# Expert answers, layer-3 projections and masks of a four-layer transformer: three stages made one, keys rotated in transposed layout

## The reference

```python
# layer 2, feed-forward: a token's expert answers, times its gate, are added
combine = gates1_s[:, None, None] * mask1[:, :, None] * loc_oh[:, None, :]
...
moe_out = jnp.einsum('sec,ecm->sm', combine, expert_out)
...
out = res_mlp_out * coef[:, :1] + moe_out * coef[:, 1:]
out = out + residual
# layer 3, attention: 16 heads of 8, rotary positions, a window of five keys
qh = (q @ Wq).reshape(Bq, Lq, N_HEADS, HDIM).transpose(0, 2, 1, 3)
kvl = kv @ Wkv
...
qh = qh * q_cos + rotate_half(qh) * q_sin
...
kh = kh * k_cos + rotate_half(kh) * k_sin
keep = (kidx[None, None, :] <= seg_id[:, :, None]) & (kidx[None, None, :] >= seg_id[:, :, None] - LOOKBACK)
scores = jnp.einsum('bhqd,bhkd->bhqk', qh, kh) * scale
scores = jnp.where(keep[:, None], scores, -jnp.inf)
attn = jax.nn.softmax(scores, axis=-1)
ctx = jnp.einsum('bhqk,bhkd->bhqd', attn, vh)
...
return out @ Wo
```

## Time and profile before

| | us |
|---|---|
| median of three runs | 3355.51 |
| profiled execution | 3358.82 |
| its span | 3357.3 |
| gather, 2532 to 2618 | 86.0 |
| tables, 2618 to 2628.4 | 10.4 |
| projections, 2628.4 to 2841 | 212.6 |
| masks and the way to the attention, 2841 to 2862 | 21 |
| attention of layer 3, 2862 to 3155 | 293 |

### The profile page before, as it was taken

How to read it: one execution, slowest core, us unless ns; L and a number is a source line. 1 busy time by engine, 2 the same in 40 slices (tenths; PEclk the granted TensorE clock), 3 DMA queues, 4 the chain that set the end, 5 groups by cost and what they waited for, 6 DMA issues and landing times. The chain is left out here.

```text
span 3357.3 us, 66661 instructions
## 1 busy us (share of the span) xinstructions
PE 2687.0 (80%) x24521; PEld 1819.8 (54%) x24556; DVE 2136.1 (64%) x5336; ACT 1249.5 (37%) x1888; POOL 441.2 (13%) x749
## 2 busy tenths in 40 slices
PE   4857599967999999999978887879790466788557
PEld 4634356645656666566645555556570355566427
DVE  6789789963555455555545777768203556789874
ACT  3658688850000000000016655545340111444264
POOL 0022200000000000000000000023216000445204
PEclk9987699988999999999987888889895677899789
DMA  3010000012121221212200000010131221000001
GB/s 87 28 58 1 11 18 13 16 51 101 51 101 51 76 76 50 101 50 79 72 8 14 14 9 9 1 34 26 50 100 50 69 56 38 3 0 0 8 0 50
DMA packets 88405, 136.92 MB, mean 41 GB/s; under 512 B 42950, under 2 KB 54598, under 8 KB 87243
## 3 DMA queue, kind: packets, MB, share of 16 engines
q1 hardware_dynamic: 80746, 114.75, 10.7%
q0 software_dynamic: 7520, 20.34, 2.0%
HBM read 117.75 MB, written 17.30 MB: 40 GB/s over the span
## 5 line engine op out<-in xcount | busy, mean ns | idle before, releaser
L1426 PE MATMUL banks<-l1f_xe,l1f_w 128*128 128x512 f32 x1024 | 486.2, 597 | 10.8 <-DVE l1f_xe L1625 10.8
L1625 DVE TENSOR_TENSOR l1f_xe<-l1f_hT,l1f_rwb 128x512 f32<-128x512 f32 x256 | 173.5, 693 | 301.2 <-PE banks L1428 278.6
L1428 PEld LDWEIGHTS banks<-l1f_w,l1f_xe 128*128 128x128 f32 x2048 | 270.7, 193 | 123.6 <-issue 123.6
L1631 DVE TENSOR_TENSOR l1f_ae<-l1f_aoT,l1f_rwb 128x512 f32<-128x512 f32 x256 | 172.8, 691 | 159.2 <-PE banks L1456 154.7
L1428 PE MATMUL banks<-l1f_w,l1f_xe 128*128 128x128 f32 x2048 | 271.6, 276 | 0.0
L1426 PEld LDWEIGHTS banks<-l1f_xe,l1f_w 128*128 128x128 f32 x1024 | 177.0, 192 | 141.1 <-issue 126.5
L1456 PE MATMUL banks<-l1f_ae,l1f_w 128*128 128x512 f32 x512 | 223.9, 596 | 1.4 <-DVE l1f_ae L1631 1.4
L1456 PEld LDWEIGHTS banks<-l1f_ae,l1f_w 128*128 128x128 f32 x512 | 96.7, 191 | 117.3 <-issue 115.1
L223 PE MATMUL banks<-consts,l3p_h 128*128 128x128 f32 x64 | 17.8, 433 | 164.8 <-DVE l3p_h L140 164.8
L214 POOL COPY x<-xn 128x512 f32 (+1 forms) x16 | 9.8, 611 | 973.2 <-DVE xn L1655 973.2
L1105 DVE TENSOR_REDUCE l2a_top<-banks 128x16 f32<-128x1024 f32 x64 | 78.4, 1224 | 65.2 <-PE banks L1052 64.7
(11 more groups left out here) (491 smaller groups left out, 6308.8 us busy)
## 6 DMA issues: line engine op xcount, KB each, us to landing
l1f_rwb<-l1f_shares SPq DMA_DIRECT2D x128, 512.0 KB, 4.5
l3p_ctx<-in_ctxT SPq DMA_DIRECT2D x32, 256.0 KB, 4.0
l0a_ctxT<-in_ctxT SPq DMA_DIRECT2D x16, 256.0 KB, 2.6
l2f_sent<-l0f_zero SPq DMA_DIRECT2D x4, 1024.0 KB, 7.0
l1a_ctxT<-in_ctxT SPq DMA_DIRECT2D x16, 256.0 KB, 2.6
l2c_ctxT<-in_ctxT SPq DMA_DIRECT2D x16, 256.0 KB, 2.6
l2e_rows<-l2f_sent SPq DMA_DIRECT2D x16, 256.0 KB, 2.8
l2f_answers<-l2e_y POOLq DMA_DIRECT2D x16, 256.0 KB, 2.7
```

The lines of the kernel that those rows point to most:

```text
L1426: pe.matmul(bank, w[:, n, e, :], xe[:, e % NB, :], start=(e == 0), stop=(e == E - 1))
L1428: last = pe.matmul(v_bank[:, D * j:D * j + D], xe[:, e % NB, P * j:P * j + P], w[:, 2, e, :], start=(e == 0 and j == 0), stop=(e == E - 1) ...
L1625: dve.tensor_tensor(xe[:, e % NB, :], hT[:, m, :], rwb[:, m, e, :], ALU.mult).then_inc(s.xe_ready, 1)
L1631: dve.tensor_tensor(ae[:, e % NB, :], aoT[:, m, :], rwb[:, m, e, :], ALU.mult).then_inc(s.ae_ready, 1)
```

## The change

The gather stage and the mask stage are taken out. Their work goes elsewhere:

- The gather, the update of x and its statistics become parts of the projections' pipeline. The DRAM tensor, the gates and the indices are allocated outside (`routed`) so that they outlive the experts' stage. The gathered rows have a ring of four groups. The root of the variance, per group, is ScalarE's (`root`), reciprocal and shift are VectorE's (`finish`), and the layer norm itself moves from VectorE to ScalarE (`norm`).
- Keys are projected as `kT` directly (weights stationary, context moving, one product of 512 columns for the keys, one for the rotated half) and rotated in that layout, with a table whose partitions are channels: `wide` is copied from the table, transposed on TensorE and copied by ScalarE into `key_trig`. The key transposes and the key store go.
- Values are projected in half columns: for each sequence two products with the same 64 tokens, one for the even and one for the odd heads, into the two halves of the partitions, and ScalarE stores them in one copy. The doubled context goes.
- The query rotation has three VectorE instructions of 128x512 instead of nine.
- All steps are written out (`behind=k.NG`), there is no hardware loop in this stage.
- POOL makes each tile's mask inside the attention (`make`), in four instructions instead of one copy.

```diff
-            pipeline(pe, k.NG, [(0, turn), (2, turn_k), (2, turn_q), (1, project)])
+            def keys(g, m):
+                pe.wait_ge(s.ctx_loaded, 16 * (g + 1))
+                wait(pe, s.k_chain, 2 * g)
+                pe.matmul(k_bank, wk[:, 0:D], ctxT[:, m % 2, :], start=True, stop=True)
+                pe.matmul(swapped_bank, wk[:, D:2 * D], ctxT[:, m % 2, :], start=True, stop=True).then_inc(s.k_psum, 1)
+
+            def values(g, m):
+                wait(pe, s.v_stored, g)
+                for q in range(SG):
+                    for p in range(2):
+                        last = pe.matmul(v_bank[64 * p:64 * p + 64, S * q:S * q + S], ctxT[:, m % 2, S * q:S * q + S],
+                                         wv[:, :].rearrange("c (a e n) -> c a e n", e=2, n=HD)[:, :, p, :], start=True, stop=True)
+                last.then_inc(s.v_psum, 1)
...
+            each_group(pe, [(0, keys), (0, values), (1, turn), (2, turn_q), (1, queries)])
...
+            def gather(g, m):
+                wait(pool, s.x_ready, g - RING4 + 1)
+                for j in range(TG):
+                    t = TG * g + j
+                    pool.indirect_dma_start(out=rows[:, m, j, :], out_offset=None, in_=kept.answers,
+                                            in_offset=bass.IndirectOffsetOnAxis(ap=kept.back[:, t:t + 1], axis=0)).then_inc(gathered[m], 16)
...
-            pipeline(act, k.NG, [(0, copy_hT), (2, store_k), (2, store_q)])
+            def root(g, m):
+                act.wait_ge(s.stats_ready, g + 1)
+                act.activation(rstd[:, m % 2, :], mv[:, m % 2, :, 1], ACT.Sqrt, bias=eps[:, 0:1]).then_inc(s.std_ready, 1)
+
+            def norm(g, m):
+                act.wait_ge(s.shift_ready, g + 1)
+                wait(act, s.hT_psum, g)
+                for j in range(TG):
+                    last = act.activation(h[:, j, :], k.x[:, TG * g + j, :], ACT.Identity, bias=shift[:, m % 2, j:j + 1],
+                                          scale=rstd[:, m % 2, j:j + 1])
+                last.then_inc(s.h_ready, 1)
...
+            each_group(act, [(1, norm), (0, store_v), (1, copy_hT), (2, store_q), (0, root)])
...
-            pipeline(dve, k.NG, [(0, norm), (1, rope_k), (1, rope_q), (1, store_v)])
+            def rope_q(g, m):
+                dve.wait_ge(s.q_psum, g + 1)
+                wait(dve, s.qT_psum, g)
+                wait(dve, s.q_roped, g)
+                src = k.banks[:, 2:4, :].rearrange("p b (t a h e) -> p (b t) a h e", t=2, a=2, e=HD)
+                for a, dst in enumerate((qr, q_part)):
+                    dve.tensor_tensor(dst[:, :, :].rearrange("p t (h e) -> p t h e", e=HD), src[:, :, a],
+                                      table[:, a, TG * g:TG * g + TG, :].unsqueeze(2).to_broadcast([P, TG, H, HD]), ALU.mult)\
+                        .then_inc(s.q_chain, 1)
+                dve.wait_ge(s.q_chain, 2 * (g + 1))
+                dve.tensor_tensor(qr[:, :, :], qr[:, :, :], q_part[:, :, :], ALU.add).then_inc(s.q_roped, 1)
...
+            each_group(dve, [(2, rope_q), (1, finish), (0, rope_k), (0, update), (0, stats)])
...
-        def copy(pool, t, par, used):
+        def make(pool, t, par, used):
             wait(pool, used, t - 1)
+            wait(pool, ready, t)
             settle(pool, k)
-            pool.tensor_copy(mask_b[:, par], masks[:, bass.ds(t, 1), :]).then_inc(ready, 1)
+            pool.tensor_tensor(away[:, :], k.count64, r.segments[:, bass.ds(t, 1)].to_broadcast([P, S]), ALU.subtract).then_inc(made, 1)
+            pool.wait_ge(made, 2 * t + 1)
+            settle(pool, k)
+            pool.tensor_scalar(far[:, :], away[:, :], float(-LOOKBACK), NEG, ALU.is_lt, ALU.mult)
+            pool.tensor_scalar(away[:, :], away[:, :], 0.0, NEG, ALU.is_gt, ALU.mult).then_inc(made, 1)
+            pool.wait_ge(made, 2 * t + 2)
+            settle(pool, k)
+            pool.tensor_tensor(mask_b[:, par], away[:, :], far[:, :], ALU.add).then_inc(ready, 1)
```

More of the change, by code:

```diff
@@ L991, in residents @@
         segments=segments and ctx.enter_context(nc.sbuf_tensor(f"{name}_segments", [P, k.NT], F32)))
-def store_v2(dve, k, r, g):
-    for p in range(2):
-        half = slice(64 * p, 64 * p + 64)
-        out = r.v2[half, bass.ds(SG * g, SG), :].rearrange("k q (j n) -> k q j n", n=HD)
-        psum = k.banks[half, 6:8, :].rearrange("k b (q j n) -> k (b q) j n", j=HD, n=2 * HD)[:, :, :, HD * p:HD * p + HD]
-        last = dve.tensor_scalar(out, psum, 0.0, None, ALU.add)
-    return last
 CORE_SEMS = ("weights x_read biased xn_ready stats_chain stats_ready mv_copied q_ready k_ready v_ready score_psum max_ready "
@@ L1926, in load, with _ @@
                 wait(sp, s.v_psum, g - 1)
-                wait(sp, s.ctx_loaded, 48 * g)
-                group = k.dram["ctxT"][:, bass.ds(g * GT, GT)]
-                sp.dma_start(ctxT[:, m, :], group).then_inc(s.ctx_loaded, 16)
-                for copy in range(2):
-                    sp.dma_start(ctx2[:, m, :, copy, :], group.rearrange("c (q n) -> c q n", n=S)).then_inc(s.ctx_loaded, 16)
-            pipeline(sp, k.NG, [(0, load)])
+                wait(sp, s.ctx_loaded, 16 * g)
+                sp.dma_start(ctxT[:, m % 2, :], k.dram["ctxT"][:, bass.ds(g * GT, GT)]).then_inc(s.ctx_loaded, 16)
+            each_group(sp, [(0, load)])
+        @block.gpsimd
+        def _(pool):
+            def gather(g, m):
[4 more added lines that the diff above has]
+                                            in_offset=bass.IndirectOffsetOnAxis(ap=kept.back[:, t:t + 1], axis=0)).then_inc(gathered[m], 16)
+            each_group(pool, [(0, gather)])
         @block.tensor
@@ L1937, in _ @@
             pe.wait_ge(s.weights, 16 * 5)
+            pe.wait_ge(s.wide_ready, 1)
+            for a in range(2):
+                last = pe.transpose(trig_bank[:, P * a:P * a + P], wide[:, a, :], k.ident)
+            last.then_inc(s.wide_psum, 1)
+            def keys(g, m):
[10 more added lines that the diff above has]
+                last.then_inc(s.v_psum, 1)
             def turn(g, m):
@@ L2071, in l3_masks @@
-def l3_masks(nc, k, r, masks):
-    with ExitStack() as ctx:
-        s = sems(nc, ctx, "l3m", "chain")
-        away = ctx.enter_context(nc.sbuf_tensor("l3m_away", [P, k.NT, S], F32))
-        far = ctx.enter_context(nc.sbuf_tensor("l3m_far", [P, k.NT, S], F32))
-        block = ctx.enter_context(nc.Block())
-        @block.vector
-        def _(dve):
-            chain = Chain(dve, s.chain)
-            chain.wait(chain.did(dve.tensor_tensor(away[:, :, :], k.count64.unsqueeze(1).to_broadcast([P, k.NT, S]),
-                                                   r.segments[:, :].unsqueeze(2).to_broadcast([P, k.NT, S]), ALU.subtract)))
-            chain.wait(chain.did(dve.tensor_scalar(far[:, :, :], away[:, :, :], float(-LOOKBACK), NEG, ALU.is_lt, ALU.mult)))
-            chain.wait(chain.did(dve.tensor_scalar(away[:, :, :], away[:, :, :], 0.0, NEG, ALU.is_gt, ALU.mult)))
-            chain.wait(chain.did(dve.tensor_tensor(masks[:, :, :], away[:, :, :], far[:, :, :], ALU.add)))
@@ new lines, in update, with stats @@
+            def update(g, m):
+                dve.wait_ge(gathered[m], 16 * TG * (g // RING4 + 1))
+                for j in range(TG):
+                    t = TG * g + j
+                    last = dve.scalar_tensor_tensor(out=k.x[:, t, :], in0=rows[:, m, j, :], scalar=kept.gate[:, t:t + 1], in1=k.x[:, t, :],
+                                                    op0=ALU.mult, op1=ALU.add)
+                last.then_inc(s.x_ready, 1)
+            def stats(g, m):
+                dve.wait_ge(s.x_ready, g + 1)
+                wait(dve, s.stats_ready, g - 1)
+                for j in range(TG):
+                    last = dve.bn_stats(bn6[:, m % 2, j, :], k.x[:, TG * g + j, :])
+                last.then_inc(s.bn_ready, 1)
+                dve.wait_ge(s.bn_ready, g + 1)
+                wait(dve, s.shift_ready, g - 1)
+                for j in range(TG):
+                    last = dve.bn_aggr(mv[:, m % 2, j, :], bn6[:, m % 2, j, :])
+                last.then_inc(s.stats_ready, 1)
@@ L2090, in phase_l3_attention @@
+            each_group(dve, [(2, rope_q), (1, finish), (0, rope_k), (0, update), (0, stats)])
+def phase_l3_attention(nc, k, kept):
     with ExitStack() as ctx:
         r = residents(nc, k, ctx, "l3", segments=True)
-        l3_projections(nc, k, r)
-        masks = ctx.enter_context(nc.sbuf_tensor("l3_masks", [P, k.NT, S], BF16))
+        l3_projections(nc, k, r, kept)
+        away = ctx.enter_context(nc.sbuf_tensor("l3_away", [P, S], F32))
+        far = ctx.enter_context(nc.sbuf_tensor("l3_far", [P, S], F32))
```

183 lines of the change are left out of this document (68 added, 115 removed).

## The result

The changed kernel took 3214.57 us (median of four runs, 3212.88 to 3218.49) against 3355.9 us before (3348.74 to 3356.46): ratio 0.9583, 95% interval 0.9572 to 0.9595. The forecast was 3193 us, with a range of 3168 to 3245; the range of its likeliest case, 3175 to 3212, was missed by 2.6 us. The sign, the mechanism and the gain of the merged stage came out; the price of the masks was twice what was forecast.

The account below looks back on a forecast made before the run. The prediction took the old projections as bound by a ring of latencies, the attention mostly by VectorE. Merged stage and barrier -178.5 us, masks +15, sum -163.5: 3358.8 becomes 3195.3 profiled, 3192 on the median's scale; predicted 3193, range 3168 to 3245.

Parts of the forecast that it names:

- likeliest case: Whole kernel: the forecast itself holds, with a time of 3175 to 3212 us; chance 0.60.
- The ring: Merged stage: query products, rotation, shift, norm, transposes and copy wait on each other in turn, 7.54 us a group against 13.3.
- Start and end: Merged stage: first query rotation about 28.3 us in, last rotation, transposes and copy 3.5; with the rounds and barrier, 178.5 saved.
- the masks' term: Attention: POOL making masks delays each of 15 joints (once in four tiles) by 1.0 us, +15 us.
- 14.9 + 3d: Attention: cycle of four tiles in us, d being POOL's added time a tile; 19.1 forecast, against 18.2 before.
- signs named: Profile after: among others, rotations 7.5 us apart, mask operations 0.25 to 0.3 each, joints 19.1 to 19.6 apart.
- (a): Attention: POOL's masks cost more, 2 to 3.5 us a tile, +45 to +110 in place of +15, about 3245; chance 0.14.
- (b): Merged stage: TensorE stays at 1.2 GHz; 3261 if in all rounds, 3216 if in a third; chance 0.10.
- (c): Merged stage: VectorE's operations stretch the gathers to 9.8 us a group, +36 us, 3229; chance 0.04.
- the rule weighed: Merged stage: VectorE's two-port copies and tensor_scalars block POOL, holding gathers only during the 6.3 us of tables.
- (d): Attention: the masks stay in POOL's slack, 3178 us; chance 0.08.
- (e): Attention: POOL's slow comparisons make it the bound of all 64 tiles; at 5.3 us a tile +235, 3415; chance 0.03.

Follow-up runs that it names:

- e9: Changed kernel with the value products issued twice in each group; 3216.37 us, ratio 0.9579 to the kernel before.
- e6: Changed kernel with the gather in a stage of its own again, ahead of the new projections; 3296.62 us, ratio 0.9828 to the kernel before.
- e11: Changed kernel with masks made beside the projections, the last stage's addition on VectorE, and VectorE's and ScalarE's steps reordered; 3160.67 us, ratio 0.9419 to the kernel before.
- e5: Changed kernel without the mask's two comparisons and one wait on POOL (result not the reference's); 3189.46 us, ratio 0.9501 to the kernel before.

## Why the prediction was right, and where it was off

**Bounds.** That the new stage is a ring of latencies held. e9 and e6 moved TensorE's and VectorE's work by about 1.1 us a group each without moving the round; e11 cut the ring and the round went to VectorE's sum. For the old projections no run tests it.

**The ring.** 7.54 forecast, 7.40 measured: from the rotation's start to the norm's 2.33 us (2604.95 to 2607.28; 2.04 + 0.35 + 0.06 forecast), norm 1.65, queries 1.99 where 1.89 was taken. Beside it little waited longer than foreseen: VectorE stood still 0.80 us before the rotation, against 0.6. The granted clock was 0.98. The forecast was 0.14 us a round too long.

**Start and end.** First query rotation 27.0 us after the first gather, 28.3 forecast into the stage (its terms add up to 28.7). The last round took 9.64 us. With no more keys and values to do, TensorE stood still 4.08 us for the norm; the granted clock was 0.82 from 2655 to 2662.5 and 0.50 from 2662.5 to 2666.4, and the last query products took 3.78 us where they took 1.99 in the loop. Together 179.9 against 178.5. That it came so near is in part luck: fourteen rounds were 2.0 us shorter in sum than forecast, and the last was 2.1 longer.

**The step that failed is the masks' term,** "I take 1.0 us for each of 15 joints: +15 us"; +31.3 was measured. Its mechanism was right: some slack, then a cycle of 14.9 + 3d. Two sizes in it were off. First d: 1.67 and not 1.4 (the terms given for it add up to 1.47). POOL's tensor_scalar with two operations on 128x64 takes 0.44 us, where I took 0.25, near the minimum of a row on four columns; the tensor_tensors (0.29, 0.32) were as priced, the waits (0.20, 0.18) a little under their 0.25. That is 3 x 0.27 x 15 = 12 us. Second, the base: 14.9 + 3d was read at a joint at full clock, but I set it against 18.2, a mean over cycles at both clocks. Like against like is 17.6 to 20.0, so even with d = 1.4 the term was (19.1 - 17.6) x 15 = 22.5 us. 15 + 7.5 + 12 = 34.5; measured are 31.3, since in the profile of before seven of 14 cycles are long ones (18.6 to 18.8), in that of after four. So two of the signs named did not come: mask operations of 0.25 to 0.3 us, and joints 19.1 to 19.6 us apart.

**What was not in the sum:** 7.4 us in the last stage of the profiled execution, from the phase in which VectorE and POOL meet there. For the profiled execution 3195.3 us were forecast, and 3212.88 came. The masks' term makes 16.3 of the difference and the last stage 8.8; the early start (6.4) and the merged stage (1.4) take some back.

**Rivals.** (a) has the right place, a dearer mask, but its d began at 2. (b) the low clock did not come, (c) neither: the 64 gathers took 949 ns on the mean, 946 before. Nor were they held beside the tables, where the rule weighed would have had it: the seven from 2528.76 to 2536.30 took 0.95 or 0.96 us each. (d) and (e) did not come; e5, with d = 0.5, shows the case of (d).
